# Decay arguments as one minimum, x times dt and the skip product on GpSimd, and an output product placed before the scores

## The chip, the cores and the metric

The kernel runs on one core of a Trainium2 chip, in one launch. The metric is the device time of one execution in microseconds; lower is better.

## The reference, cut to what matters

The program is a network of two layers over 1024 tokens of 512 values: attention, a linear layer, then a state space mixer (below), then an expert layer. The change is in the mixer and in the small tables that are made ahead of it. There are 128 heads of 64 values, in 8 groups, and the tokens are two sequences of 512.

```python
cum = jnp.cumsum(dA.reshape(b, nc, CS, H), axis=2)
Ldec = jnp.exp(cum[:, :, :, None, :] - cum[:, :, None, :, :])   # masked: j <= i
scores = jnp.einsum('bcihn,bcjhn->bcijh', Cc, Bc) * Ldec * dtc[:, :, None, :, :]
y_intra = jnp.einsum('bcijh,bcjhp->bcihp', scores, xc)
dlast = jnp.exp(cum[:, :, -1:, :] - cum)
states = jnp.einsum('bcjh,bcjhn,bcjhp->bchpn', dtc * dlast, Bc, xc)
y_inter = jnp.einsum('bcihn,bchpn->bcihp', Cc * jnp.exp(cum)[..., None], prev)
y = (y_intra + y_inter).reshape(b, l, H, P) + Dp[None, None, :, None] * x
...
g = y * jax.nn.silu(gate)
g = (gg * jax.lax.rsqrt(var + EPS)).reshape(b, l, INTER) * norm_w
return g @ out_w.T
```

## The kernel before, in words

The mixer works through 8 groups of heads, and each group through 16 steps. A step k takes 8 heads (half of a group) and one chunk of 128 tokens: half = k // 8 and c = k mod 8. Four chunks make a sequence. A step with c mod 4 not 0 carries a state in from the chunk before ("carrying"), one with c mod 4 not 3 feeds a state on. The steps of all groups are numbered through as s.

Each engine has a queue written out by hand, and semaphores order the queues against each other. In a step they do this:

- TensorE: the gate's product (into p_gate_intra), the product of the carried state (p_inter_state, L1668), the convolution's projection (p_mix) for the chunks that come later, the output product of the step before (p_out, 12 products of 128x512), the new state (L1682), the transposition of x (p_flip), the scores times x (L1693), and a product that sums the squares of the y of the step before (L1603, into the bank of p_inter_state). L102 is the line of a helper that issues all the large products.
- ScalarE: eight Exps of the decays (L1780), the high part of y (L1745), y's squares (L1751), the emptying of p_flip into x_tokens (L1738), the gate's and the convolution's activations and the convolution's first tap (L785).
- VectorE: `arguments(s + 1)` for the next step's decays (L1927), `skip_part` (L1973 and L1976), the state's decay and sum (L2036, L2075, L2077), the other three taps of the convolution (L807), `make_y` (y's sum L1984, times the gate L1989), the low part of y (L1937) and the reads of the sum of squares (L1944, L1946). In the first step of a half (c = 0) it also splits four pieces of the output weights (w_out, L1905).
- GpSimd: the decays times the scores of the chunk (`decayed`, L2156), x times the state's factors (`to_state`, L2147), the two sums of squares (L2131, L2133), the low parts of the gate's and the convolution's weights.

The matrix of a step and head holds exp(min(cum_i - cum_j, 0)) times dt_j. Before, VectorE formed the difference head by head, with one column of the table as minimum and subtrahend, and the logarithm of dt was the bias of the Exp. Ahead of the mixer, the tables of cum and of log dt are made and written; `end_logs` forms cum at the chunk's end minus cum plus log dt for the states, once a group.

In the last step of a half (c = 7) there is no new state and no transposition behind the convolution's products, and the output product of the step before stands behind the scores; in the other steps it stands ahead of the state.

## Time and profile before

| what | value |
|---|---|
| time, median of 3 runs | 2126.28 us (2123.61 to 2127.76) |
| time of the profiled execution | 2117.76 us |
| its span | 2115.8 us |
| granted TensorE clock, mean share | 0.982 |
| TensorE matmul busy | 1973.0 us (93%) |
| VectorE busy | 1797.9 us (85%) |
| ScalarE busy | 1447.2 us (68%) |
| GpSimd busy | 1054.1 us (50%) |

The span runs from the first to the last instruction in the trace, and the time is that of the whole execution. The mixer takes most of it, from about 402 to 2045 us of the span; a full group takes 205 us. Busy shares are means over the whole program, in which the stages ahead of the mixer and behind it have other limits. In rows of the trace, PE is TensorE, PEld its weight loads, DVE is VectorE, ACT is ScalarE and POOL is GpSimd; L and a number is the line of the kernel, and buffer numbers of tiles are left out, so that wq_t names the decays' buffer, p_gate_intra the bank of the gate's and of the scores' products, and p_inter_state that of the carried state, of the new state and of the sum of squares.

### The profile page before, as it was taken

Reading aid. Unit: us, or ns where it says so; the run is one execution under the profiler, and the core shown is the slowest. Engines: PE = TensorE matmul, PEld = TensorE weight load, DVE = VectorE, ACT = ScalarE, POOL = GpSimd, SP = SyncE. Lnnn points to the kernel's source line nnn. Section 1 sums busy time; section 2 is a strip of 40 time slices with the busy share of each in tenths; the row PEclk is TensorE's granted clock in tenths of the full one; section 3 lists DMA queues with packets and bytes.
Section 4 is the critical chain, followed back from the end, with each engine's and each line's share of the span. In section 5 each row is a group of like instructions: output and inputs, shape, how many; then the busy total and the mean of one; then the engine's idle time right before and its main releaser. Section 6 shows DMA issues by size and latency. Waiting matters only on the chain.

```text
span 2115.8 us, 34810 instructions
## 1 busy us (share of the span) xinstructions
PE 1973.0 (93%) x11288; PEld 1528.3 (72%) x11288; DVE 1797.9 (85%) x4144; ACT 1447.2 (68%) x2756; POOL 1054.1 (50%) x1033
## 2 busy tenths in 40 slices
PE   8899896799999999999999999999999999999878
PEld 4666575587777777777777777777777777777655
DVE  5777674589899989998998999989999998999976
ACT  1566624577778777777787777777877777877621
POOL 4555240245555555546554645465546555654541
PEclk9999997899999999999999999999999999999989
DMA  4000010233222313232323232223232322222201
GB/s 169 2 0 0 1 56 19 85 110 110 71 79 96 124 65 106 76 115 66 109 86 104 86 89 95 86 85 89 96 98 72 108 92 90 81 90 80 96 19 40
DMA packets 125713, 166.09 MB, mean 79 GB/s; under 512 B 37777, under 2 KB 88977, under 8 KB 121330
## 3 DMA queue, kind: packets, MB, share of 16 engines
q1 hardware_dynamic: 125554, 164.11, 24.2%
q8 instruction: 83, 1.36, 0.3%
q14 instruction: 76, 0.62, 0.1%
HBM read 159.88 MB, written 4.20 MB: 78 GB/s over the span
## 4 chain that ended last, share of the span: by engine, by line
DVE 30%; PE 27%; ACT 21%; issue 7%; POOL 2%; SPq 0%; DMA 0%; ACTq 0%; POOLq 0%; DVEq 0%
DVE conv L807 10%; PE p_mix L102 6%; PE p_out L102 6%; DVE wq_t L1927 6%; PE p_gate_intra L102 5%; ACT wq_t L1780 4%; ACT L1790 3%; ACT L1780 3%; DVE w_out L1905 2%; PE p_gate_intra L1693 2%; DVE x_skip L1976 2%; ACT conv L785 2%; POOL wq_t L2156 2%; ACT x_and_gate L1790 2%; DVE p_gate_intra L1984 2%
## 5 line engine op out<-in xcount | busy, mean ns | idle before, releaser
L2156 POOL TENSOR_TENSOR wq_t<-wq_t,cb 128x1024 f32<-128x1024 f32 x128 | 309.3, 2416 | 386.0 <-ACT wq_t L1780 374.8
L102 PE MATMUL p_out<-w_out,yT 128*128 128x512 f32 x1536 | 383.7, 400 | 11.2 <-DVE yT L1937 11.2
L1927 DVE TENSOR_SCALAR wq_t<-cum_all,tables_in 128x128 f32<-128x128 f32 x1024 | 359.2, 422 | 4.1 <-DMA cum_all<-cum_rows 4.1
L807 DVE SCALAR_TENSOR_TENSOR conv<-p_mix,unit_small,conv 128x511 f32<-128x511 f32 (+2 forms) x384 | 287.0, 748 | 83.9 <-ACT conv L785 72.8
L102 PE MATMUL p_gate_intra<-x_high,w_gate 128*128 128x512 f32 x1024 | 351.5, 404 | 6.1 <-ACT x_and_gate L1790 4.9
L102 PE MATMUL p_mix<-x_high,w_x 128*128 128x512 f32 x1024 | 351.6, 405 | 1.4 <-DVE x_low L1155 1.4
L102 PEld LDWEIGHTS p_out<-w_out,yT 128*128 128x128 f32 x1536 | 290.7, 191 | 82.6 <-DVE yT L1937 15.0
L1780 ACT ACTIVATE wq_t<-wq_t,tables_in 128x128 f32<-128x128 f32 x1024 | 326.1, 390 | 4.9 <-DVE wq_t L1927 3.4
L795 ACT ACTIVATE x_and_gate<-conv 128x512 f32<-128x512 f32 x128 | 80.9, 632 | 259.4 <-DVE conv L807 259.2
L102 PEld LDWEIGHTS p_gate_intra<-x_high,w_gate 128*128 128x128 f32 x1024 | 194.3, 190 | 45.6 <-issue 6.1
L102 PEld LDWEIGHTS p_mix<-x_high,w_x 128*128 128x128 f32 x1024 | 193.7, 189 | 39.9 <-DVE x_low L1155 1.8
L102 PE MATMUL p_gate_intra<-x_low,w_gate 128*128 128x512 f32 x512 | 201.8, 394 | 0.0
L102 PE MATMUL p_mix<-x_low,w_x 128*128 128x512 f32 x512 | 201.0, 393 | 0.0
L2147 POOL TENSOR_TENSOR x_to_state<-x_tokens,group_exps 128x512 f32<-128x512 f32 x96 | 101.2, 1054 | 171.1 <-ACT x_tokens L1738 171.1
L1693 PE MATMUL p_gate_intra<-wq_t,x_tokens 128*64 128x128 f32 x2048 | 140.9, 280 | 29.9 <-POOL wq_t L2156 29.9
L1780 ACT ACT_TABLE_LOAD x118 | 151.4, 1283 | 2.1
L1693 PEld LDWEIGHTS p_gate_intra<-wq_t,x_tokens 128*64 128x64 f32 x2048 | 109.9, 137 | 58.5 <-POOL wq_t L2156 36.6
L1790 ACT ACT_TABLE_LOAD x110 | 141.1, 1283 | 2.0
L826 POOL TENSOR_TENSOR w_x<-w_raw_tiles,w_x 128x512 fp32r<-128x512 f32 x64 | 83.0, 1297 | 112.9 <-DVE w_x L815 112.9
L476 DVE CUSTOM_DVE_ANT_0 pF<-pF,row_mask 128x128 f32<-128x128 f32 (+3 forms) x256 | 115.8, 530 | 18.5 <-PE pF L293 18.5
L1668 PEld LDWEIGHTS p_inter_state<-bc_channels,state 128*128 128x128 f32 x768 | 99.5, 194 | 43.6 <-issue 38.6
L1668 PE MATMUL p_inter_state<-bc_channels,state 128*128 128x128 f32 x768 | 105.3, 281 | 27.0 <-DVE mean_square L1946 17.5
(242 smaller groups left out, 4216.7 us busy)
## 6 DMA issues: line engine op xcount, KB each, us to landing
cum_all<-cum_rows SPq DMA_DIRECT2D x128, 512.0 KB, 3.8
exp_cum<-exp_rows SPq DMA_DIRECT2D x192, 128.0 KB, 3.4
w_staged<-in_w_gate SPq DMA_DIRECT2D x16, 1024.0 KB, 5.5
w_raw_tiles<-in_w_x SPq DMA_DIRECT2D x64, 256.0 KB, 3.0
w_staged<-in_w_out SPq DMA_DIRECT2D x16, 1024.0 KB, 4.9
w_raw_tiles<-in_w_bc SPq DMA_DIRECT2D x16, 256.0 KB, 5.3
x<-in_x SPq DMA_DIRECT2D x1, 2048.0 KB, 18.6
out<-x_and_gate SPq DMA_DIRECT2D x8, 256.0 KB, 2.0
```

The costliest lines, as they stand in the source:

```text
L102: last = pe.matmul(dst, left[a](k), right[b](k), start=k == 0 and n_ == 0, stop=stop and k == tiles - 1 and n_ == 2)
L476: m = dve.tensor_tensor_reduce(pF[:, b, n_ * wide:(n_ + 1) * wide], pF[:, b, n_ * wide:(n_ + 1) * wide], row_mask[:, CPS * P - wide:], 1.0 ...
L795: act.activation(dst, src, ACT.Silu).then_inc(self.conv_done, 1)
L807: m = dve.scalar_tensor_tensor(self.conv[:, par, back:], self.p_mix[:, bank, 0:SEQ - back], w[:, TAPS - 1 - back:TAPS - back], self.conv[: ...
L826: pool.tensor_tensor(self.wx[:, 1, j], self.raw[:, j % 2], self.wx[:, 0, j].bitcast(F32), ALU.subtract).then_inc(self.x_w_split, 1)
L1668: m = pe.matmul(p_inter[:, j * P:(j + 1) * P], state[:, 2 * j:2 * j + 2].rearrange("p h e -> p (h e)"), BC[:, 1, cols], start=True, stop=True)
L1693: m = pe.matmul(p_intra[a * HEAD_P:(a + 1) * HEAD_P, j * P:(j + 1) * P], xtok[:, k % 2, h], decay[:, k % 2, h], start=True, stop=True)
L1780: m = act.activation(decay[:, k % 2, h], decay[:, k % 2, h], ACT.Exp, bias=tab[:, s // STEPS % 2, 1, c, head:head + 1])
L1790: act.activation(tile_of(SG, phase, j), p_gate.rearrange("p (q t) -> p q t", t=P), ACT.Silu).then_inc(sg_done, 1)
L1927: m = dve.tensor_scalar(decay[:, k % 2, h], cumB[:, h], own, own, ALU.min, ALU.subtract)
L2147: pool.tensor_tensor(xs[:], xtok[:, k % 2], over(exps[:, 0, c, mine], HEAD_P), ALU.mult).then_inc(xs_done, 1)
L2156: pool.tensor_tensor(decay[:, k % 2], decay[:, k % 2], cb[:, c].unsqueeze(1).to_broadcast([P, UNIT_HEADS, P]), ALU.mult).then_inc(decay_do ...
```

## The change

- The argument of a step is one VectorE minimum of cum_i and cum_j over 128x1024 (8 heads); minus cum_j is the bias of the Exp. The table of log dt becomes one of dt, and the Ln that made it goes.
- dt is multiplied into x: GpSimd's `to_scores` forms x_dt from x_tokens in every step, and the scores' products take x_dt. The state's factors get dt from `dt_end`, once a group. x_tokens has one buffer in place of two.
- `end_logs` moves from VectorE to GpSimd, and also forms minus cum.
- GpSimd forms the skip product (x times D) in one operation, behind the decayed scores and ahead of the sums of squares. In carrying steps VectorE adds the carried part with one operation, `add_skip`, behind the taps (c below 7) or ahead of y's sum (c = 7). TensorE's carried product and sum of squares wait for that addition; before, they waited for `skip_part`.
- At c = 7 the output product of the step before stands ahead of the scores.

```diff
@@ layer 0's end: the tables @@
-                act.wait_ge(const2, 3)
-                act.wait_ge(stats_done, 4 * CHUNKS + 1)
-                act.activation(log_dt[:], dt[:], ACT.Ln, bias=head_small[:, 3:4]).then_inc(soft, 1)
...
@@ TensorE @@
-                                wait(pe, xskip_done, s)
+                                wait(pe, skip_sum, n_carries(g, k))
...
-                            if c < CHUNKS - 1:
-                                project_out(*before)
+                            project_out(*before)
...
-                        pe.wait_ge(flip_out, s + 1)
+                        pe.wait_ge(xdt_done, s + 1)
...
-                        if c == CHUNKS - 1:
-                            project_out(*before)
                         if before:
-                            wait(pe, xskip_done, s + 1)
+                            wait(pe, skip_sum, n_carries(g, k + 1))
                             square_sums(*before, p_inter)
@@ ScalarE @@
-                        m = act.activation(decay[:, k % 2, h], decay[:, k % 2, h], ACT.Exp, 
-                                           bias=tab[:, s // STEPS % 2, 1, c, head:head + 1])
+                        m = act.activation(decay[:, k % 2, h], decay[:, k % 2, h], ACT.Exp,
+                                           bias=neg[:, s // STEPS % 2, c, head:head + 1])
@@ VectorE @@
-                    for h in range(UNIT_HEADS):
-                        head = half * UNIT_HEADS + h
-                        own = tab[:, s // STEPS % 2, 0, c, head:head + 1]
-                        m = dve.tensor_scalar(decay[:, k % 2, h], cumB[:, h], own, own, ALU.min, ALU.subtract)
-                    m.then_inc(arg_done, 1)
-
-                end_logs(0)
+                    dve.tensor_tensor(decay[:, k % 2], cumB[:], over(tab[:, s // STEPS % 2, 0, c, mine], P),
+                                      ALU.min).then_inc(arg_done, 1)
...
-                            dve.wait_ge(carried_done, nc_ + 1)
-                            skip_part(g, k)
...
+                        def add_skip():
+                            if carries(c):
+                                dve.wait_ge(carried_done, n_carries(g, k) + 1)
+                                dve.wait_ge(xskip_done, s + 1)
+                                skipped = xskip[:].rearrange("p j t -> p (j t)")
+                                dve.tensor_tensor(skipped, p_inter[:], skipped, ALU.add).then_inc(skip_sum, 1)
...
                         if c == CHUNKS - 1:
+                            add_skip()
                             make_y(g, k)
                             taps_of(events)
...
+                        add_skip()
                         if feeds(c):
@@ GpSimd @@
+                def skip_part(g, k, first):
+
+                    half, c = divmod(k, CHUNKS)
+                    if c % CPS == 0:
+                        pool.wait_ge(conv_done, len(PLAN.first) if first and k == 0 else
+                                     PLAN.ready(g, k - 1, ("x", UT - 1, c // CPS)))
+                    wait(pool, y_sum, step(g, k))
+                    pool.tensor_tensor(xskip[:], chunk_of(X, c // CPS, c % CPS), over(skip[:, g % 2, half], P),
+                                       ALU.mult).then_inc(xskip_done, 1)
...
+                        def to_scores():
+                            wait(pool, intra_done, s)
+                            pool.tensor_tensor(xdt[:], xtok[:], over(tab[:, g % 2, 1, c, mine], HEAD_P),
+                                               ALU.mult).then_inc(xdt_done, 1)
+
+                        if k == 0:
+                            dt_end(g)
                         if c % CPS == 0:
-                            decayed()
+                            decayed(g, k)
+                        pool.wait_ge(flip_out, s + 1)
                         if feeds(c):
-                            pool.wait_ge(flip_out, s + 1)
                             to_state()
+                        to_scores()
+                        if not (first and k < 2) and older[1] >= CHUNKS:
+                            inverse_rms(*older)
                         if c % CPS:
-                            decayed()
+                            decayed(g, k)
+                        skip_part(g, k, first)
+                        if k == STEPS - 2 and not last:
+                            end_logs(g + 1)
                         if not (first and k == 0):
                             sum_squares(s - 1)
```

TensorE's queue at the last step of a half, from the last convolution product to the first gate product, before:

```order
L102 MATMUL p_mix<-x_low,w_x 128x512
L102 MATMUL p_mix<-x_high,w_x 128x512
L1693 MATMUL p_gate_intra<-wq_t,x_tokens 64x128 x8
L102 MATMUL p_out<-w_out,yT 128x512 x12
L1603 MATMUL p_inter_state<-one_column,y_squares 128x1
L102 MATMUL p_gate_intra<-x_high,w_gate 128x512
```

and after the change:

```order
L102 MATMUL p_mix<-x_low,w_x 128x512
L102 MATMUL p_mix<-x_high,w_x 128x512
L102 MATMUL p_out<-w_out,yT 128x512 x12
L1689 MATMUL p_gate_intra<-wq_t,x_dt 64x128 x8
L1600 MATMUL p_inter_state<-one_column,y_squares 128x1
L102 MATMUL p_gate_intra<-x_high,w_gate 128x512
```

The output product went from behind the scores to ahead of them; the scores' line is now L1689, and they take x_dt.

GpSimd's queue at the first step of the second half (k = 8), from the decays to the sums of squares of the step before, and on to the decays of k = 9, before:

```order
L2156 TENSOR_TENSOR wq_t<-wq_t,cb 128x1024
L2147 TENSOR_TENSOR x_to_state<-x_tokens,group_exps 128x512
L2131 TENSOR_TENSOR y_squares<-y_squares 128x256
L2133 TENSOR_TENSOR y_squares<-y_squares 128x128
L2147 TENSOR_TENSOR x_to_state<-x_tokens,group_exps 128x512
L2156 TENSOR_TENSOR wq_t<-wq_t,cb 128x1024
L2131 TENSOR_TENSOR y_squares<-y_squares 128x256
```

and after the change:

```order
L2110 TENSOR_TENSOR wq_t<-wq_t,cb 128x1024
L2151 TENSOR_TENSOR x_to_state<-x_tokens,group_dt_end 128x512
L2156 TENSOR_TENSOR x_dt<-x_tokens,tables_in 128x512
L2101 TENSOR_TENSOR x_skip<-x_and_gate,skip_in 128x512
L2137 TENSOR_TENSOR y_squares<-y_squares 128x256
L2139 TENSOR_TENSOR y_squares<-y_squares 128x128
L2151 TENSOR_TENSOR x_to_state<-x_tokens,group_dt_end 128x512
L2156 TENSOR_TENSOR x_dt<-x_tokens,tables_in 128x512
L2110 TENSOR_TENSOR wq_t<-wq_t,cb 128x1024
L2101 TENSOR_TENSOR x_skip<-x_and_gate,skip_in 128x512
```

x_dt (L2156 there, whose number before was that of the decays) and the skip product (L2101) came in ahead of the two sums of squares, which are L2137 and L2139 after.

VectorE's queue in step k = 9, a carrying one, from the arguments of the next step to y's sum, before:

```order
L1927 TENSOR_SCALAR wq_t<-cum_all,tables_in 128x128 x8
L1937 TENSOR_TENSOR yT<-p_gate_intra,yT 128x512
L2029 TENSOR_TENSOR p_inter_state<-p_inter_state,exp_cum 128x512
L1973 SCALAR_TENSOR_TENSOR x_skip<-x_and_gate,skip_in,p_inter_state 128x128 x4
L2036 TENSOR_TENSOR state<-state,group_exps 128x512
L819 CAST w_bc<-w_raw_tiles 128x512
L807 SCALAR_TENSOR_TENSOR conv<-p_mix,unit_small,conv 128x511
L807 SCALAR_TENSOR_TENSOR conv<-p_mix,unit_small,conv 128x510
L807 SCALAR_TENSOR_TENSOR conv<-p_mix,unit_small,conv 128x509
L2075 TENSOR_TENSOR state<-p_inter_state,state 128x512
L1984 TENSOR_TENSOR p_gate_intra<-p_gate_intra,x_skip 128x512
```

and after the change:

```order
L1910 TENSOR_TENSOR wq_t<-cum_all,tables_in 128x1024
L1919 TENSOR_TENSOR yT<-p_gate_intra,yT 128x512
L2001 TENSOR_TENSOR p_inter_state<-p_inter_state,exp_cum 128x512
L2006 TENSOR_TENSOR state<-state,group_exps 128x512
L819 CAST w_bc<-w_raw_tiles 128x512
L807 SCALAR_TENSOR_TENSOR conv<-p_mix,unit_small,conv 128x511
L807 SCALAR_TENSOR_TENSOR conv<-p_mix,unit_small,conv 128x510
L807 SCALAR_TENSOR_TENSOR conv<-p_mix,unit_small,conv 128x509
L2018 TENSOR_TENSOR x_skip<-p_inter_state,x_skip 128x512
L2048 TENSOR_TENSOR state<-p_inter_state,state 128x512
L1956 TENSOR_TENSOR p_gate_intra<-p_gate_intra,x_skip 128x512
```

The eight operations of the arguments became one (L1910), the four of the skip went from behind the carried product, and the addition L2018 stands behind the three taps, ahead of the state's sum (L2048) and y's sum (L1956).

## Rows read from the trace of the kernel before

**Rows 1.** Windows, two groups; columns as in the line on top.
```profile
core 0: us, PE busy (x) PEld busy (x) DVE busy (x) ACT busy (x) POOL busy (x), PEclk, DMA share, GB/s
980.03:1185.22 205.19, 198.50 (x1122) 157.70 (x1121) 187.79 (x401) 158.36 (x299) 113.69 (x95) 1.00 0.29 92
1390.38:1597.13 206.75, 199.96 (x1121) 158.82 (x1121) 187.88 (x401) 158.35 (x299) 113.73 (x95) 0.99 0.29 91
```

**Rows 2.** Timeline, TensorE, one group: start, us, engine, line, tiles, [idle before <-releaser].
```profile
1011.61 1.09 PE L1693 MATMUL p_gate_intra<-wq_t,x_tokens 128*64 128x128 f32 x16 [2.31 <-POOL wq_t L2156]
...
1034.16 1.13 PE L1668 MATMUL p_inter_state<-bc_channels,state 128*128 128x128 f32 x8 [0.71 <-DVE mean_square L1946]
...
1112.46 1.09 PE L1693 MATMUL p_gate_intra<-wq_t,x_tokens 128*64 128x128 f32 x16 [1.49 <-POOL wq_t L2156]
...
1132.13 1.13 PE L1668 MATMUL p_inter_state<-bc_channels,state 128*128 128x128 f32 x8 [1.17 <-DVE sum_squares L1944]
```

**Rows 3.** Costliest groups: busy us, mean ns of one | idle before.
```profile
L1927 DVE TENSOR_SCALAR wq_t<-cum_all,tables_in 128x128 f32<-128x128 f32 x1024 | 359.2, 422 | 4.1 <-DMA cum_all<-cum_rows 4.1
...
L2156 POOL TENSOR_TENSOR wq_t<-wq_t,cb 128x1024 f32<-128x1024 f32 x128 | 309.3, 2416 | 386.0 <-ACT wq_t L1780 374.8
...
L2147 POOL TENSOR_TENSOR x_to_state<-x_tokens,group_exps 128x512 f32<-128x512 f32 x96 | 101.2, 1054 | 171.1 <-ACT x_tokens L1738 171.1
...
L1973 DVE SCALAR_TENSOR_TENSOR x_skip<-x_and_gate,skip_in,p_inter_state 128x128 f32<-128x128 f32 x384 | 107.8, 343 | 3.4
```

**Rows 4.** Timeline, VectorE, ahead of the mixer and in a step.
```profile
356.34 1.23 DVE L1187 SCALAR_TENSOR_TENSOR dt<-dt,dt_abs 128x1024 f32<-128x1024 f32 x1 [8.48 <-ACT dt_abs L1102]
...
1035.11 2.14 DVE L1927 TENSOR_SCALAR wq_t<-cum_all,tables_in 128x128 f32<-128x128 f32 x8
```

**Rows 5.** Timeline, TensorE and VectorE, around the ends of two halves.
```profile
1018.78 2.92 PE L102 MATMUL p_out<-w_out,yT 128*128 128x512 f32 x12
...
1113.61 0.70 DVE L1984 TENSOR_TENSOR p_gate_intra<-p_gate_intra,x_skip 128x512 f32<-128x512 f32 x1 [2.32 <-PE p_gate_intra L1693]
...
1117.26 0.69 DVE L1937 TENSOR_TENSOR yT<-p_gate_intra,yT 128x512 fp32r<-128x512 f32 x1
...
1119.36 2.92 PE L102 MATMUL p_out<-w_out,yT 128*128 128x512 f32 x12
```

**Rows 6.** Timeline, VectorE, GpSimd and TensorE, first steps of two halves.
```profile
1024.71 2.73 DVE L1905 SCALAR_TENSOR_TENSOR w_out<-w_staged,unit_small,w_out 128x512 fp32r<-128x512 f32 x4
...
1024.78 2.97 POOL L2133 TENSOR_TENSOR y_squares<-y_squares 128x128 f32<-128x128 f32 x1
...
1123.99 3.70 DVE L1905 SCALAR_TENSOR_TENSOR w_out<-w_staged,unit_small,w_out 128x512 fp32r<-128x512 f32 x4 [0.95 <-ACT w_out L1729]
...
1124.43 1.18 POOL L2131 TENSOR_TENSOR y_squares<-y_squares 128x256 f32<-128x256 f32 x1
...
1126.71 1.09 PE L1693 MATMUL p_gate_intra<-wq_t,x_tokens 128*64 128x128 f32 x16
```

**Rows 7.** Timeline, ScalarE, VectorE and TensorE, step k = 9.
```profile
1138.15 0.77 ACT L785 ACTIVATE conv<-p_mix,unit_small 128x512 f32<-128x512 f32 x1
...
1139.69 2.30 DVE L807 SCALAR_TENSOR_TENSOR conv<-p_mix,unit_small,conv 128x511 f32<-128x511 f32 x3
...
1141.03 0.38 PE L1603 MATMUL p_inter_state<-one_column,y_squares 128*128 128x1 f32 x2
```

**Rows 8.** Timeline, ScalarE and TensorE, ahead of the mixer's first step.
```profile
358.45 1.15 ACT L1105 ACTIVATE dt<-dt,head_small 128x1024 f32<-128x1024 f32 x1 [2.14 <-DVE dt_abs L1189]
...
398.94 0.47 PE L102 MATMUL p_gate_intra<-x_high,w_gate 128*128 128x512 f32 x1 [2.50 <-ACT x_and_gate L1790]
```

**Rows 9.** Timeline, VectorE and TensorE, one of the last steps.
```profile
2002.48 4.51 DVE L1927 TENSOR_SCALAR wq_t<-cum_all,tables_in 128x128 f32<-128x128 f32 x8
...
2007.64 4.35 PE L102 MATMUL p_out<-w_out,yT 128*128 128x512 f32 x12 [3.67 <-DVE yT L1937]
```

**Rows 10.** Timeline, TensorE, an output product at a later half's end.
```profile
1422.99 4.62 PE L102 MATMUL p_out<-w_out,yT 128*128 128x512 f32 x12
```

More of the change, by code:

```diff
@@ L1964, in out_sum @@
                                              ALU.mult, ALU.add).then_inc(acc_done, 1)
-                def skip_part(g, k):
-                    half, c = divmod(k, CHUNKS)
-                    src = chunk_of(X, c // CPS, c % CPS)
-                    for j in range(UT):
-                        gain = skip[:, g % 2, half, j:j + 1]
-                        if carries(c):
-                            m = dve.scalar_tensor_tensor(xskip[:, j], src[:, j], gain, p_inter[:, j * P:(j + 1) * P],
-                                                         ALU.mult, ALU.add)
-                        else:
-                            m = dve.tensor_scalar(xskip[:, j], src[:, j], gain, None, ALU.mult)
-                    m.then_inc(xskip_done, 1)
                 def make_y(g, k):
```

80 lines of the change are left out of this document (39 added, 41 removed).

## The prediction

> **What bounds the kernel now.** I read the busy time by stage first, because the page's busy shares are means over stages with different limits. In one group of the mixer TensorE is busy 198.50 of 205.19 us [rows 1]; VectorE has 187.79, ScalarE 158.36 and GpSimd 113.69. TensorE is the bound, and a group can gain no more than 205.19 - 198.50 = 6.7 us. Then I read TensorE's own timeline through that group for its waits. Four of them carry most of the 6.7 [rows 2]: the scores wait for the decays on GpSimd at the two ends of a half (2.31 and 1.49), and the first carrying product of a half waits for VectorE's read of the mean square or the sum of squares (0.71 at k = 1, 1.17 at k = 9). Elsewhere in the group no wait of TensorE reaches 0.7. So time taken off VectorE is worth something only in so far as it reaches these four places, the start of the mixer, or its last steps.
>
> The profiled execution took 2117.76 us, with a span of 2115.8; the median of the runs shown is 2126.28, that is 8.5 more. The sum below is made against 2117.76 and then put on the median by adding its difference to 2126.28. About 0.2% (4 us) is what a measurement of this kernel can tell from no change.
>
> **The arguments.** Eight operations of 0.422 us become one minimum over 128x1024 [rows 3]. The nearest operation of that size with two SBUF inputs took 1.23 us; eight old ones undisturbed took 2.14 [rows 4]. Per step 359.2/128 = 2.81 becomes 1.23 to 1.6. In a steady group this is off the path: the Exps on ScalarE use arguments made a step earlier, and their number and form stay. Worth there: 0.
>
> **The skip term.** Four operations of 0.343 us [rows 3] leave VectorE in a carrying step, and one addition of 128x512 comes in (0.70 by the additions of that size [rows 5]). GpSimd gets one 128x512 product more for the skip, and another for x times dt. Priced by x_to_state, 1.054 us each [rows 3], this is 16 x 2.1 = 34 us in a group, on top of 113.7: 148 of 205, so GpSimd does not become the bound by its sum. The product with dt stands ahead of the decays in most steps, and the decays behind it wait 386.0/128 = 3.0 us a step for ScalarE anyway [rows 3], which covers its 1.05; ScalarE's copy into x_tokens, now one buffer, waits for the product of the step before, which is long past. Both at 0, unless that cover goes. The step without it is c = 0, where the decays stand first.
>
> **The half's end (c = 7).** Before, TensorE ends the convolution's products at 1112.46 - 1.49 = 1110.97 and begins the next step's output product at 1119.36: 8.4 us; at the group's end 1011.61 - 2.31 = 1009.30 to 1018.78: 9.5 [rows 2, 5]. After, the older output product (2.92) stands first and covers the wait for the decays; the scores follow (1.09); from their end at 1113.55 VectorE needs until 1117.26 + 0.69 = 1117.95, 4.4 us, to have y split [rows 5], with y's sum, gate, three taps and the split in a row. 2.92 + 1.09 + 4.4 = 8.4. The wait thus moves to the next output product, which no older product now covers. At k = 7 I get 0, at k = 15 a gain of 1.1: **-1.1 us a group**, bounds -3.8 (both waits gone) and 0.
>
> **The first step of a half (c = 0).** VectorE splits w_out in four operations while GpSimd works on the same step. At k = 8 the four took 3.70 us, with a sum of squares on GpSimd in between; at k = 0 they took 2.73 in one run, and a GpSimd operation of 128x128 beside them took 2.97 [rows 6]. So the two keep each other out, and at k = 8 VectorE lost 3.70 - 2.73 = 0.97 to it. After the change GpSimd has two operations of 1.05 more there, ahead of the two sums of squares. If they come in between the splits, the splits end up to 2.1 later. Behind the splits stand the taps, the state's copy, y and the read of the sum of squares, for which the carrying product of k = 9 waits already, so this delay lands on TensorE in full. One more GpSimd operation let in is +1.0, two are +2.1, none is 0. I take +1.0 at k = 8, because the two sums of squares then fall behind the splits. At k = 0 the splits go from 2.73 to 3.70 + 1.0 = 4.7, so 2.0 longer, but can begin 1.3 sooner (they start 5.93 after the output product there, 4.63 at k = 8 [rows 5, 6], as VectorE has less ahead of them): +0.7. Together **+1.7 us a group**, bounds -1.7 and +3.9.
>
> The Trainium skill ("SBUF — State Buffer", section "SBUF: two separate sides") says that a VectorE operation with two SBUF inputs and a GpSimd operation take a shared pair of ports in turn as an exclusive lock, each for its whole instruction. By that rule all of GpSimd's new operations would alternate with the splits, and the +1.7 would be +3.9. The trace agrees at k = 8 and not at k = 0, where VectorE went through four operations in a row.
>
> **The sums of squares.** The product that sums y's squares writes into the bank that the skip term is added from, so it waits for the new addition, which stands behind the step's taps; before, it waited for the skip operations ahead of the taps. At k = 9 it ran at 1141.03 while the taps ended at 1139.69 + 2.30 = 1141.99 [rows 7]. After the change VectorE reaches the taps sooner, but ScalarE's first tap ends only at 1138.15 + 0.77 = 1138.92: taps to 1141.2, addition to 1141.9, so TensorE waits 0.9. What is queued behind on TensorE is the gate's product, and behind that everything. In the other steps TensorE is later against the taps; I put them at 0.3 together, from 0 to 2. **+1.2 us a group**.
>
> **Sum in the groups.** -1.1 + 1.7 + 1.2 = +1.8. The first and last of eight groups have only part of this: 7.5 x 1.8 = +13.5.
>
> **Ahead of the mixer.** The Ln of dt goes (1.15, with ScalarE on the path [rows 8]): -1. The first gate product after the convolution's waits 2.50 for ScalarE [rows 8], which waited for the first arguments; one operation in place of eight, and the end logs on another engine, take up to 2.5 off, but the end logs now stand on GpSimd ahead of the gate weights: -2. **-3**, bounds 0 and -5.
>
> **The last steps.** With no further group to prepare, TensorE is not full. The output product waits 3.67 us for y's split, which stands behind arguments that took 4.51 [rows 9]; the same pair comes once more some 17 us later. The arguments become 1.23 alone, or 3.4 if GpSimd's two new operations keep them out: -1.1 to -3.3, I take -2.3 twice, and -1.4 for the output product ahead of the last scores, near the 1.49 of the half's end [rows 2]. **-6**, bounds -2 and -10.
>
> **In all** 13.5 - 3 - 6 = +4.5 us: 2122 in an execution like the profiled one, and on the median **2131**.
>
> **The rivals.**
> *A, the sum above*: 45%. Its own range is 2121 to 2141.
> *B, VectorE keeps the upper hand at c = 0*: the splits run as at k = 0 (2.73, GpSimd kept out, [rows 6]). Then k = 0 loses its wait of 0.71. At k = 8 x times dt comes only after 1123.99 + 2.73 + 1.05 = 1127.8, where the scores ran at 1126.71 [rows 6], so the scores lose 1.1 and this eats the 1.17 gained at k = 9. The taps are 1.0 sooner, and the 0.9 at the sum of squares goes. A group is -1.1 - 0.7 - 0.1 + 0.2 = -1.7, times 7.5 is -13, with -9 outside -22: 2104. For it: the row of 2.97; against it: the 3.70 at k = 8, where GpSimd came in. It decides at one GpSimd operation fewer between the splits. 30%.
> *C, all four waits go*: 7.5 x 6.7 = 50, and 9 outside: 2067. Against it: y's chain of 4.4 has nothing taken out. 5%.
> *D, the new waits lower TensorE's clock*: after the 2.31 wait at the end of one half the output product ran 4.62 instead of 2.92 [rows 10], and that group took 206.75 instead of 205.19 [rows 1]. With 1.6 more at both halves of a group, 15 times, 24 comes on top of A: 2155. Against it: the other waits of this length left the clock alone. 10%.
> *E, nothing of it is seen*: gains at start and end are as large as the losses, 7.5 x 1.2 = 9 against 9, or hidden: 2126. 10%.
>
> **The numbers.** B, C and the lower end of A (0.06) are faster: 0.41. E and the middle of A (0.15) are the same: 0.25. D and the upper part of A (0.24) are slower: 0.34. The range reaches to B and into D, 2100 to 2150, and leaves out C, most of D and a little of B.
>
> **What would show it.** In the profile after: the minimum at 1.2 to 1.6 us; no wait of the scores for the decays at c = 7, but one of the output product for y's split in the next step; the four w_out splits at 4 to 5 us in both halves; the sum of squares waiting about 0.9 for the new addition at k = 9; group times of 206 to 208 us. Splits of 2.7 us and groups near 203.5 would show B. What would make it wrong most easily is the placing of GpSimd's two new operations against VectorE's, at c = 0 and in the steps where I put their effect at nothing.

## The result and the profile after

The changed kernel took 2147.55 us (median of 4, 2144.84 to 2151.23) against 2127.02 us of the kernel before (median of 4): a ratio of 1.0102 (95% interval 1.0090 to 1.0114), 20.5 us slower. The prediction was 2131, +4.5, with a range of 2100 to 2150. The side and the range were right; the size was a quarter of what was measured, and 2147.55 lies outside the 2121 to 2141 that the prediction gave to its own sum. The side was in part luck: by the prediction's own chances "faster" (0.41) stood ahead of "slower" (0.34).

The page's busy line after the change, as a whole:

```profile
span 2146.7 us, 33910 instructions
PE 1986.8 (93%) x11288; PEld 1542.5 (72%) x11288; DVE 1601.3 (75%) x2815; ACT 1445.1 (67%) x2755; POOL 1391.0 (65%) x1313
```

VectorE lost 197 us of work and GpSimd took on 337. The kernel is nevertheless slower, because TensorE is the bound and it waits longer.

The spans of the two profiled executions differ by 30.9 us, ten more than the medians. Part of that lies ahead of everything that was changed. The timeline of TensorE shows one product of the linear layer that precedes the mixer's tables, and then the mixer's first scores, before:

```profile
305.59 0.39 PE L102 MATMUL pM<-w_lin_low,srcT 128*128 128x512 f32 x1
...
416.32 1.09 PE L1693 MATMUL p_gate_intra<-wq_t,x_tokens 128*64 128x128 f32 x16
```

and after:

```profile
315.61 0.39 PE L102 MATMUL pM<-w_lin_low,srcT 128*128 128x512 f32 x1
...
423.78 1.09 PE L1689 MATMUL p_gate_intra<-wq_t,x_dt 128*64 128x128 f32 x16
```

Ten us are lost ahead of that product, where the code is the same; the shown execution of before was a quick one there, and it also lies 8.5 under the median of before. What the change did is the other 20.9, and that is the difference of the medians.

A group of the mixer (windows; busy us and instructions of each engine, granted clock, DMA share, GB/s):

```profile
1672.33:1880.69 208.36, 199.43 (x1121) 159.18 (x1120) 163.49 (x235) 158.23 (x298) 155.85 (x130) 0.99 0.29 90
```

A group went from 205.19 [rows 1] to 208.36 us, +3.2, and eight of them make 25. TensorE was idle 6.7 us in it before and is idle 8.9 now; the other 0.9 is that its products take 199.4 in place of 198.5, in this group at a lower clock for a part of it (below). These are its waits in that group, from its timeline:

```profile
1678.18 1.13 PE L1665 MATMUL p_inter_state<-bc_channels,state 128*128 128x128 f32 x8 [1.12 <-DVE mean_square L1928]
...
1712.14 0.38 PE L1600 MATMUL p_inter_state<-one_column,y_squares 128*128 128x1 f32 x2 [1.62 <-DVE x_skip L2018]
...
1763.66 3.04 PE L102 MATMUL p_out<-w_out,yT 128*128 128x512 f32 x12 [1.26 <-DVE yT L1919]
...
1773.87 0.35 PE L1600 MATMUL p_inter_state<-one_column,y_squares 128*128 128x1 f32 x2 [1.65 <-issue]
...
1787.83 0.38 PE L1600 MATMUL p_inter_state<-one_column,y_squares 128*128 128x1 f32 x2 [0.45 <-DVE x_skip L2018]
...
1813.78 0.38 PE L1600 MATMUL p_inter_state<-one_column,y_squares 128*128 128x1 f32 x2 [0.62 <-DVE x_skip L2018]
...
1870.54 2.99 PE L102 MATMUL p_out<-w_out,yT 128*128 128x512 f32 x12 [1.99 <-DVE attn L1937]
```

Against [rows 2]: the scores' waits for the decays (2.31 and 1.49) are gone, and the output products of the next step wait in their place (1.26 for y's split at k = 8, 1.99 at the next group's k = 0, there for VectorE's read of the output product before). The sum of squares, which waited for nobody, waits at k = 3, 8, 9 and 11.

Behind the wait of 1.65 the granted clock was at its lower level (1.2 GHz) for a part of the gate's products. In an earlier group the same wait (1.66) left the clock at 2.4 GHz. The same products there and here (windows, columns as above):

```profile
730.71:734.52 3.81, 2.99 (x14) 2.18 (x14) 3.63 (x8) 2.10 (x4) 0.44 (x1) 1.00 0.00 0
1774.09:1778.51 4.42, 4.42 (x15) 3.47 (x15) 4.24 (x8) 2.71 (x4) 1.05 (x2) 0.61 0.00 0
```

At the upper level the products are done sooner, and the carried product of k = 9 then waits 3.81 - 2.99 = 0.82 for VectorE; after it the sum of squares waits 0.95 instead of 0.45:

```profile
744.44 0.38 PE L1600 MATMUL p_inter_state<-one_column,y_squares 128*128 128x1 f32 x2 [0.95 <-DVE x_skip L2018]
```

So a group at the upper level throughout has 10.3 us of waits and one like the group shown has 8.9 and slower products, and both take 208.4.

The new operations, from the costliest groups (busy us, mean ns | idle before):

```profile
L1910 DVE TENSOR_TENSOR wq_t<-cum_all,tables_in 128x1024 f32<-128x1024 f32 x128 | 211.7, 1654 | 4.1 <-DMA cum_all<-cum_rows 3.1
L2156 POOL TENSOR_TENSOR x_dt<-x_tokens,tables_in 128x512 f32<-128x512 f32 x128 | 179.7, 1404 | 27.0 <-ACT x_tokens L1731 23.9
L2101 POOL TENSOR_TENSOR x_skip<-x_and_gate,skip_in 128x512 f32<-128x512 f32 x128 | 155.0, 1211 | 0.0
```

All three are longer than the rows of before let expect (1.23, 1.05, 1.05), because VectorE and GpSimd keep each other out. The first step of the second half shows it (timeline of VectorE and GpSimd):

```profile
1762.66 2.39 POOL L2110 TENSOR_TENSOR wq_t<-wq_t,cb 128x1024 f32<-128x1024 f32 x1 [5.01 <-ACT wq_t L1774]
...
1763.59 2.55 DVE L1910 TENSOR_TENSOR wq_t<-cum_all,tables_in 128x1024 f32<-128x1024 f32 x1
...
1768.41 5.05 DVE L1899 SCALAR_TENSOR_TENSOR w_out<-w_staged,unit_small,w_out 128x512 fp32r<-128x512 f32 x4 [2.28 <-ACT w_out L1723]
...
1768.85 1.49 POOL L2156 TENSOR_TENSOR x_dt<-x_tokens,tables_in 128x512 f32<-128x512 f32 x1
...
1770.30 1.48 POOL L2101 TENSOR_TENSOR x_skip<-x_and_gate,skip_in 128x512 f32<-128x512 f32 x1
1771.75 1.16 POOL L2137 TENSOR_TENSOR y_squares<-y_squares 128x256 f32<-128x256 f32 x1
```

The minimum starts during the decays and ends 1.09 us after they end at 1765.05. The four splits of w_out take 5.05 (3.70 before, [rows 6]), and GpSimd's three operations take 1.2 to 1.5 each beside them: they take turns. The sums of squares come behind both, which is TensorE's wait of 1.65 at 1773.87.

The Trainium skill ("SBUF — State Buffer", section "SBUF: two separate sides") has a VectorE operation with two SBUF inputs and a GpSimd operation that reads SBUF shut each other out for a whole instruction, whichever starts first. These rows agree with that. The four splits at k = 0, which took 2.73 in every group of the kernel before, take 4.6 here in every group but the first.

### The profile page after: what moved, and what is told of

Read it like the earlier page. It is cut to its first block, busy times and chain, and to the rows that moved or that the text cites. A ratio compares the mean times of both kernels' runs of the same rounds, so it can differ in the third digit from the quotient of the medians.

```text
span 2146.7 us, 33910 instructions
## 1 busy us (share of the span) xinstructions
PE 1986.8 (93%) x11288; PEld 1542.5 (72%) x11288; DVE 1601.3 (75%) x2815; ACT 1445.1 (67%) x2755; POOL 1391.0 (65%) x1313
## 3 DMA queue, kind: packets, MB, share of 16 engines
q1 hardware_dynamic: 125554, 164.11, 23.9%
## 4 chain that ended last, share of the span: by engine, by line
PE 53%; DVE 17%; ACT 12%; issue 4%; POOL 1%; SPq 0%; DMA 0%; ACTq 0%; POOLq 0%; DVEq 0%
PE p_mix L102 13%; PE p_out L102 12%; PE p_gate_intra L102 12%; DVE conv L807 8%; PE p_gate_intra L1689 4%; DVE w_out L1899 3%; PE p_inter_state L1665 3%; ACT wq_t L1774 2%; PE p_inter_state L1678 2%; PE pM L102 2%; PE p_flip L1583 2%; ACT L1774 2%; ACT L1784 1%; PE p_inter_state L1600 1%; ACT conv L785 1%
## 5 line engine op out<-in xcount | busy, mean ns | idle before, releaser
L2110 POOL TENSOR_TENSOR wq_t<-wq_t,cb 128x1024 f32<-128x1024 f32 x128 | 331.2, 2587 | 235.0 <-ACT wq_t L1774 203.2
L102 PEld LDWEIGHTS p_out<-w_out,yT 128*128 128x128 f32 x1536 | 292.6, 192 | 96.6 <-issue 16.6
L102 PE MATMUL p_gate_intra<-x_high,w_gate 128*128 128x512 f32 x1024 | 355.8, 409 | 5.8 <-POOL w_gate L2083 3.4
L1774 ACT ACTIVATE wq_t<-wq_t,minus_cum 128x128 f32<-128x128 f32 x1024 | 326.0, 390 | 1.4
L1910 DVE TENSOR_TENSOR wq_t<-cum_all,tables_in 128x1024 f32<-128x1024 f32 x128 | 211.7, 1654 | 4.1 <-DMA cum_all<-cum_rows 3.1
L2156 POOL TENSOR_TENSOR x_dt<-x_tokens,tables_in 128x512 f32<-128x512 f32 x128 | 179.7, 1404 | 27.0 <-ACT x_tokens L1731 23.9
L2151 POOL TENSOR_TENSOR x_to_state<-x_tokens,group_dt_end 128x512 f32<-128x512 f32 x96 | 107.3, 1117 | 118.4 <-ACT x_tokens L1731 118.4
L2101 POOL TENSOR_TENSOR x_skip<-x_and_gate,skip_in 128x512 f32<-128x512 f32 x128 | 155.0, 1211 | 0.0
L1689 PE MATMUL p_gate_intra<-wq_t,x_dt 128*64 128x128 f32 x2048 | 140.1, 279 | 0.0
L1689 PEld LDWEIGHTS p_gate_intra<-wq_t,x_dt 128*64 128x64 f32 x2048 | 109.2, 136 | 27.7 <-issue 27.7
```

The source lines that it names most:

```text
L102: last = pe.matmul(dst, left[a](k), right[b](k), start=k == 0 and n_ == 0, stop=stop and k == tiles - 1 and n_ == 2)
L1689: m = pe.matmul(p_intra[a * HEAD_P:(a + 1) * HEAD_P, j * P:(j + 1) * P], xdt[:, h], decay[:, k % 2, h], start=True, stop=True)
L1774: m = act.activation(decay[:, k % 2, h], decay[:, k % 2, h], ACT.Exp, bias=neg[:, s // STEPS % 2, c, head:head + 1])
L1910: dve.tensor_tensor(decay[:, k % 2], cumB[:], over(tab[:, s // STEPS % 2, 0, c, mine], P), ALU.min).then_inc(arg_done, 1)
L2101: pool.tensor_tensor(xskip[:], chunk_of(X, c // CPS, c % CPS), over(skip[:, g % 2, half], P), ALU.mult).then_inc(xskip_done, 1)
L2110: pool.tensor_tensor(decay[:, k % 2], decay[:, k % 2], cb[:, c].unsqueeze(1).to_broadcast([P, UNIT_HEADS, P]), ALU.mult).then_inc(decay_do ...
```

## The experiments

Each was timed in turn with the kernel before, in five rounds; the ratios are to that. "The changed kernel" is the one above.

**Output product behind the scores again**

```diff
-                            project_out(*before)
+                            if c < CHUNKS - 1:
+                                project_out(*before)
...
                         m.then_inc(intra_done, 1)
+                        if c == CHUNKS - 1:
+                            project_out(*before)
```

> The changed kernel (2147.6 us) with only the output product put back behind the scores at c = 7. Theory: the reorder is about neutral, since it trades the scores' waits for the decays (3.8 us a group before) for waits of the next output product (1.26 and 1.99 us a group in the changed kernel); so 2144 to 2154 us, and the waits for the decays are back in the trace. Rival: the reorder itself costs, because the product now waits behind VectorE's read of the one before; then 2132 to 2140 us.

Measured: 2132.88 us, ratio 1.0028 (1.0017 to 1.0039), 14.7 us below the changed kernel. The rival's range was right; the theory was right only in that waits for the decays come back, and they are fewer than it had them. The view of waits (engine, tile and line waited for: us in all, times, longest) has for TensorE in the changed kernel

```profile
PE p_inter_state L1600 <- DVE x_skip L2018: 23.9, 32, 1.6
...
PE p_out L102 <- DVE attn L1937: 13.9, 7, 2.0
PE p_out L102 <- DVE yT L1919: 12.3, 11, 1.3
```

and without the reorder

```profile
PE p_inter_state L1600 <- DVE x_skip L2021: 24.1, 32, 1.7
...
PE p_gate_intra L1690 <- POOL wq_t L2113: 11.3, 9, 2.2
...
PE p_out L102 <- DVE yT L1922: 2.2, 3, 0.8
```

The output products lose 24 of 26 us of waiting, and the scores wait 11.3 us for the decays, not the 29.9 that they waited before the change: at k = 7 not at all, at k = 15 for 1.28. The other parts of the change had already brought the decays forward, so the reorder had little left to cover: per group it puts 1.26 + 1.99 of waits in the place of 1.28.

**Skip term on VectorE again, reorder kept**

```diff
-                                wait(pe, skip_sum, n_carries(g, k))
+                                wait(pe, xskip_done, s)
...
+                            dve.wait_ge(carried_done, nc_ + 1)
+                            skip_part(g, k)
...
-                        add_skip()
...
-                        skip_part(g, k, first)
```

> The changed kernel with the skip term back on VectorE in its four operations ahead of the taps, TensorE waiting for those as before; the minimum, x times dt on GpSimd and the reorder stay. Theory: the skip's move is the larger part of the loss, through the sum of squares that waits for the addition behind the taps (about 1.7 us a group) and through one GpSimd operation fewer beside the w_out splits (about 1 us a group): 2122 to 2132 us. Rival: x times dt on GpSimd is what costs, by keeping VectorE out of its port: 2140 us or more.

Measured: 2130.94 us, ratio 1.0018 (1.0008 to 1.0028), 16.6 us below the changed kernel. The theory holds for the skip's move as a whole.

**The minimum alone, on the kernel before**

```diff
+                    dve.tensor_tensor(neg[:, g % 2], tab[:, g % 2, 1], tab[:, g % 2, 0], ALU.subtract).then_inc(logs_done, 1)
...
+                    dve.tensor_tensor(decay[:, k % 2], cumB[:], over(tab[:, s // STEPS % 2, 0, c, mine], P),
+                                      ALU.min).then_inc(arg_done, 1)
```

> The kernel before (2127 us) with the one minimum alone: dt stays in the exponent, the bias of the Exp is log dt minus cum from one more 128x128 subtraction a group; no x times dt, no move of the skip term or of the output product. Theory: TensorE is the bound, so the minimum gives only what it takes off the start, the last steps and the first step of a half: 2112 to 2122 us. Rival: the arguments on VectorE are hidden everywhere: 2124 to 2130 us.

Here log dt is added to minus cum in single precision, where a large cum rounds it off, so this kernel computes with a changed dt; its time is that of the same operations. Measured: 2115.37 us, ratio 0.9944 (0.9930 to 0.9958), as the theory had it. By the traces the last group gives 6.8 us of it (188.3 to 181.5) and the six full groups 4.3 together.

**Sums of squares ahead of the skip product at c = 0**

```diff
-                        skip_part(g, k, first)
+                        if c:
+                            skip_part(g, k, first)
...
                             sum_squares(s - 1)
+                        if not c:
+                            skip_part(g, k, first)
```

> The changed kernel with GpSimd's skip product behind the sums of squares in the first step of a half only. Theory: the order of GpSimd's operations beside the w_out splits sets the wait at k = 8 (1.65 us at the sum of squares in the changed kernel); the splits end about 0.7 us sooner there: 2138 to 2144 us. Rival: the splits are kept out for as long by whatever GpSimd does next: within 3 us of 2147.6.

Measured: 2143.58 us, ratio 1.0078 (1.0064 to 1.0092), 4 us below the changed kernel. The waits of 1.65 at the sum of squares go, and 1.7 come back at the next carried product, which waits for VectorE behind the splits.

**The same without the reorder** (this edit and the first together)

> The changed kernel without the reorder (2132.9 us), with the skip product behind the sums of squares in the first step of a half; the addition stays behind the taps. Theory: the skip's move costs in two places, beside the w_out splits (some 4 us in all, as in the kernel with the reorder, 2147.6 to 2143.6) and through the sum of squares that waits for the addition (the rest): 2127 to 2131 us, which leaves some 13 us of the 18 to 2115 for the addition's place. Rival: the first step of a half is the larger part: 2115 to 2122 us.

Measured: 2123.57 us, ratio 0.9988 (0.9979 to 0.9997), 9.3 us below the kernel without the reorder alone. It lies between the two expectations: the first step of a half is worth about as much as the place of the addition.

**Minimum, x times dt and end logs alone** (the edits of the first two experiments together)

> The changed kernel without the reorder at c = 7 and with the skip term on VectorE as before: what stays of the change is the minimum, x times dt and the end logs on GpSimd. Theory: the two losses lie in different places (the output product's waits at c = 7; the sum of squares and the w_out splits elsewhere), so they add: 2147.6 - 14.7 - 16.6 = 2116, from 2112 to 2121 us, near the minimum alone (2115.4). Rival: both take from the same slack, or x times dt costs on its own: 2124 us or more.

Measured: 2115.00 us, ratio 0.9948 (0.9935 to 0.9961). The two losses add up (2147.6 - 14.7 - 16.6 = 2116), so the reorder and the skip term's move are what makes the changed kernel slower, and x times dt on GpSimd costs nothing that can be seen beside the 2115.4 of the minimum alone. What is left of the waits for the decays in a group (timeline):

```profile
1735.19 1.09 PE L1690 MATMUL p_gate_intra<-wq_t,x_dt 128*64 128x128 f32 x16 [0.90 <-POOL wq_t L2110]
...
1840.16 1.09 PE L1690 MATMUL p_gate_intra<-wq_t,x_dt 128*64 128x128 f32 x16 [1.72 <-POOL wq_t L2110]
```

**Addition of the skip term ahead of the taps, no reorder**

```diff
+                        add_skip()
                         if c == 0 and not (first and k == 0):
                             out_low_part(g * 2 + half, half)
                         taps_of(events)
...
-                        add_skip()
```

> The changed kernel without the reorder (2132.9 us), with the addition of the skip term ahead of the taps instead of behind them; GpSimd's order is untouched. Theory: the place of the addition makes the sum of squares wait (24 us in all in that kernel), so 2117 to 2125 us. Rival: the addition now waits for GpSimd's skip product, which stands behind the decays, and holds the taps back: 2130 us or more.

Measured: 2246.47 us, ratio 1.0561 (1.0546 to 1.0576). The rival, and by far more than it said: VectorE's waits have

```profile
DVE x_skip L2021 <- POOL x_skip L2104: 258.4, 96, 3.4
```

that is 2.7 us in each of the 96 carrying steps, with the taps and all of the next step's x behind it. The place behind the taps is the dear one for TensorE and the safe one for VectorE.

**And GpSimd's skip product ahead of the decays**

```diff
                         if c % CPS:
+                            skip_part(g, k, first)
                             decayed(g, k)
-                        skip_part(g, k, first)
+                        elif c:
+                            skip_part(g, k, first)
...
+                        if not c:
+                            skip_part(g, k, first)
```

> As the kernel with the addition ahead of the taps, and GpSimd's skip product ahead of the decays where these wait for ScalarE anyway, and behind the sums of squares in the first step of a half. Theory: with the skip product ready early nothing waits for it, and VectorE keeps the time it was spared: 2108 to 2118 us. Rival: the decays come 1.05 us later and the scores wait for them at c = 7: 2120 to 2132 us.

Measured: 2134.94 us, ratio 1.0038 (1.0024 to 1.0051): the waits of the sum of squares for the addition are gone, and the decays are late instead, as the rival said; the time is 3 us above the rival's range.

**The same, but behind the decays at c = 7**

```diff
-                        if c % CPS:
+                        if c % CPS and c < CHUNKS - 1:
                             skip_part(g, k, first)
                             decayed(g, k)
                         elif c:
+                            if c % CPS:
+                                decayed(g, k)
                             skip_part(g, k, first)
```

> The kernel with the skip product ahead of the decays (2134.9 us), but at c = 7 behind them. Theory: its wait of the scores for the decays at the group's end (2.66 us, and the output product at the lower clock behind it) comes from the skip product ahead of the decays at that step, and goes: 2110 to 2122 us. Rival: the decays are late there because ScalarE is, whatever stands ahead of them on GpSimd: 2130 us or more.

Measured: 2120.79 us, ratio 0.9973 (0.9961 to 0.9985). The scores at the group's end, in the kernel with the skip product ahead of the decays everywhere:

```profile
1854.38 1.36 PE L1690 MATMUL p_gate_intra<-wq_t,x_dt 128*64 128x128 f32 x16 [2.66 <-POOL wq_t L2113]
```

and in this one:

```profile
1838.63 1.09 PE L1690 MATMUL p_gate_intra<-wq_t,x_dt 128*64 128x128 f32 x16 [1.66 <-POOL wq_t L2113]
```

The output product behind these scores takes 4.31 us there and 3.03 here; its clock is shown in the last section. One GpSimd operation ahead of the decays costs 1.0 of waiting and then 1.3 at the lower clock. The theory holds. Even so, it is 6 us more than with the skip term on VectorE (2115.0).

**The reorder alone, on the kernel before**

```diff
-                            if c < CHUNKS - 1:
-                                project_out(*before)
+                            project_out(*before)
...
-                        if c == CHUNKS - 1:
-                            project_out(*before)
```

> The kernel before (2127 us) with the reorder at c = 7 alone. Theory: there the decays are late by 1.5 to 2.3 us at that place, so the reorder covers a wait that exists and gives it back as waits of the next output product: neutral, 2121 to 2130 us. Rival: it costs as in the changed kernel, where it was worth 14.7 us: 2136 to 2144 us.

Measured: 2131.3 us, ratio 1.0025 (1.0014 to 1.0035): a loss of about 5 us, just outside the theory's range and well short of the rival's. The windows of the six full groups and of the last one, before (first two lines) and with the reorder:

```profile
618.54:1851.11 1232.57, 1192.18 (x6721) 947.30 (x6720) 1126.44 (x2400) 950.17 (x1788) 682.37 (x564) 1.00 0.29 92
1851.11:2039.38 188.27, 160.71 (x911) 126.56 (x910) 168.64 (x363) 126.91 (x248) 89.55 (x78) 0.93 0.24 80
625.81:1861.04 1235.23, 1196.11 (x6721) 947.63 (x6720) 1121.27 (x2401) 949.03 (x1788) 669.70 (x564) 1.00 0.29 91
1861.04:2053.29 192.25, 166.07 (x922) 130.35 (x922) 169.47 (x364) 127.08 (x248) 91.96 (x80) 0.93 0.24 78
```

A full group goes from 205.4 to 205.9 on the mean, so there the theory nearly held. The last group loses 4.0, with one output product more in it than before; 1.1 of that comes back behind its last scores (75.3 us to the end, from 76.4).

**x times dt on VectorE, from the bank** (on the kernel with minimum and x times dt)

```diff
-                    act.activation(xtok[:].rearrange("p h e -> p (h e)"), p_flip[:], ACT.Copy).then_inc(flip_out, 1)
...
+                    dve.tensor_tensor(xdt[:], p_flip[:].rearrange("p (h e) -> p h e", e=HEAD_P),
+                                      over(tab[:, g % 2, 1, c, mine], HEAD_P), ALU.mult).then_inc(xdt_done, 1)
...
-                            pool.tensor_tensor(xs[:], xtok[:], over(dtend[:, c, mine], HEAD_P),
+                            pool.tensor_tensor(xs[:], xdt[:], over(exps[:, 0, c, mine], HEAD_P),
```

> The kernel with the minimum and x times dt alone (2115.0 us), with x times dt formed by VectorE straight from the transposed x in its bank, so that ScalarE's copy and one GpSimd operation a step go, and the state's factor is multiplied into that. Theory: ScalarE and GpSimd, which make the decays late at c = 7, lose 0.6 and 1.05 us a step, and VectorE gains 0.7: 2104 to 2114 us. Rival: VectorE's product stands behind y's gate and is waited for by TensorE or GpSimd: 2118 us or more.

Measured: 2080.41 us, ratio 0.9781 (0.9767 to 0.9794). This is 46 us below the kernel before, the best of all, and some 24 us below the theory's range, so the theory's prices do not explain it. A group of this kernel (windows, columns as above):

```profile
1621.86:1822.02 200.16, 197.13 (x1122) 158.07 (x1121) 172.60 (x303) 151.68 (x282) 122.22 (x96) 1.00 0.30 94
```

TensorE's idle time in a group is 3.0 us, from 6.7 in the kernel before.

**The same with ScalarE's copy back**

```diff
+                    act.activation(xtok[:].rearrange("p h e -> p (h e)"), p_flip[:], ACT.Copy).then_inc(flip_out, 1)
...
-                    dve.wait_ge(flip_done, step(g, k) + 1)
+                    dve.wait_ge(flip_out, step(g, k) + 1)
...
-                    dve.tensor_tensor(xdt[:], p_flip[:].rearrange("p (h e) -> p h e", e=HEAD_P),
+                    dve.tensor_tensor(xdt[:], xtok[:],
```

> The fastest kernel so far (2080.4 us), but with ScalarE's copy of the transposed x back, and VectorE's product with dt reading that copy instead of the bank. Theory: ScalarE, which is on the way to the decays, is what the copy's removal relieved, and most of the 35 us between 2115.0 and 2080.4 goes again: 2100 to 2118 us. Rival: taking the product off GpSimd was worth it, and ScalarE's copy is hidden: 2080 to 2092 us.

Measured: 2114.91 us, ratio 0.9958 (0.9945 to 0.9972). The theory's range is right: without the copy's removal, taking the product off GpSimd is worth nothing. Its reason, ScalarE on the way to the decays, is not what the traces show. TensorE's waits with the copy back:

```profile
PE p_inter_state L1664 <- DVE mean_square L1930: 29.6, 24, 5.0
...
PE p_inter_state L1678 <- POOL x_to_state L2160: 12.1, 17, 1.7
...
PE p_gate_intra L1689 <- POOL wq_t L2125: 7.3, 16, 1.5
```

and without it:

```profile
PE p_inter_state L1663 <- DVE mean_square L1918: 19.9, 10, 5.0
...
PE p_gate_intra L1688 <- POOL wq_t L2113: 5.2, 8, 1.8
...
PE p_inter_state L1677 <- POOL x_to_state L2148: 1.0, 1, 1.0
```

The waits for the state's x (11.1) and for VectorE's mean square (9.7) go with the copy, and those for the decays by only 2.1. The two kernels also differ in VectorE's product itself, which reads the bank or x_tokens (costliest groups, without the copy and with it):

```profile
L1960 DVE TENSOR_TENSOR x_dt<-p_flip,tables_in 128x512 f32<-128x512 f32 x128 | 87.3, 682 | 9.5 <-PE p_flip L1581 9.5
L1972 DVE TENSOR_TENSOR x_dt<-x_tokens,tables_in 128x512 f32<-128x512 f32 x128 | 129.6, 1013 | 21.1 <-ACT x_tokens L1733 20.9
```

Whether it is ScalarE's 0.6 us a step, the shorter way from the transposed x to the scores and the state, or the 0.33 that VectorE's product is shorter from the bank is not told apart; all three go with the copy.

## Why the prediction was right and wrong, point by point

**The bound and the form of the sum** were right: TensorE bounds the groups, VectorE's spared 197 us are worth nothing by themselves, and the time is made at a handful of waits.

**The arguments** came out at 1.65 on the mean, just above the 1.6 given, and GpSimd in a group at 155.9 instead of 148, both for taking turns. The minimum alone gains 11.7 us (2127 to 2115.4), of which 0.7 on the mean in a full group, where 0 was forecast. Nothing else of the change helps on balance.

**The half's end** was mis-sized, by half a microsecond a group. The term was -1.1 a group; the waits there went from 2.31 + 1.49 to 1.26 + 1.99, which is -0.55. The wait moved to the next output product as forecast. But at k = 15 I let that product wait for y's split alone. It also waits for VectorE to read the one before (the wait of 1.99), which stands behind y's split in VectorE's queue. And the question of what the half's end would be without the reorder was not asked. The wait to be covered was taken from the trace of before, but the decays were to come earlier by the change's other parts: without the reorder they are late by 0 and 1.28, not 1.49 and 2.31. So the reorder by itself cost 14.7 us in the changed kernel, and about 5 in the kernel before, where half of it lies in the last group.

**The first step of a half** was predicted at +1.7 a group, with splits of 4.7. The splits take 5.05 at k = 8, and 4.58 at k = 0 (3.70 and 2.73 before). The waits of a full group at the upper clock give +1.7 as well: 1.66 at k = 8 and 0.82 at k = 9 where 1.17 was, and 1.16 at k = 1 where 0.77 was. GpSimd's new operations did come in between the splits in both halves, which the prediction priced at up to +3.9; the splits grew by 1.35 and 1.86. That this agrees so closely is luck: the second half has 1.3 of it and the first 0.4, for 1.0 and 0.7, and the mechanism was in part another. At k = 8 the sum of squares waits (1.65) for GpSimd's sums, which stand behind the new products, and the carried product of k = 9 then waits less or not at all. The wait that I named comes back (1.7) when the sums are put first; without the reorder that order is worth 9.3 us, 1.2 a group.

**The sums of squares** are the step that failed in the groups: 1.2 was predicted, with 0.9 at k = 9 and 0.3 in all other steps together (from 0 to 2), for which no rows were read. At k = 9 the wait is 0.95 at the upper clock, as predicted. But it is 0.22 at k = 1, 1.61 at k = 3 and 0.60 at k = 11, that is 2.4 for the 0.3; over the program the waits on the addition are 23.9 us. About 1.0 of this takes the place of old waits at k = 4 and 13, so the term is +2.4 a group instead of +1.2. Against the skip term on VectorE the net loss is less: the kernel with the sums first and no reorder takes 2123.6 and the one with the skip term on VectorE 2115.0, which is 8.6 or 1.1 a group. In their traces the waits on the addition, less those that they replace, are 2.3 a group, and the waits for the decays at the half's ends are 1.3 shorter (1.3 against 0.9 + 1.7). What VectorE was spared did bring the decays forward, and the place of the addition cost more.

**Ahead of the mixer**: -3 was predicted. From the product in the linear layer to the first scores it is now 423.78 - 315.61 = 108.2 us; before it was 416.32 - 305.59 = 110.7. That is -2.5.

**The last steps** are the other step that failed: -6 was predicted, with -2.3 twice and -1.4 for the output product ahead of the last scores. The pair came out. From the scores at 1996.54 to those at 2031.91 it was 35.4 us, and it is now 30.2 (2029.96 to 2060.13), which is -5.2; its output products wait 0.83 instead of 3.67 [rows 9]:

```profile
2039.09 5.32 PE L102 MATMUL p_out<-w_out,yT 128*128 128x512 f32 x12 [0.83 <-DVE yT L1919]
```

The last half's end did not. Before:

```profile
2039.38 1.97 PE L1693 MATMUL p_gate_intra<-wq_t,x_tokens 128*64 128x128 f32 x16 [1.97 <-POOL wq_t L2156]
```

and after:

```profile
2066.17 3.83 PE L102 MATMUL p_out<-w_out,yT 128*128 128x512 f32 x12
2069.94 1.09 PE L1689 MATMUL p_gate_intra<-wq_t,x_dt 128*64 128x128 f32 x16
```

The wait of 1.97 is gone, but the output product that stands in its place runs 3.83 us, partly at the lower clock. From the scores before these to the last scores it is 9.8 us (2060.13 to 2069.94), from 7.5; and what stands behind the last scores is no shorter for it (76.8 us, from 76.4). That is +2.7 for the -1.4, and in all -2.5 for -6.

**In all**, the mixer takes 1646.2 us from its first to its last scores, from 1623.1. Its six full groups and its last one after the change (windows; those of before stand with the reorder alone):

```profile
628.94:1880.69 1251.75, 1194.21 (x6721) 952.83 (x6720) 979.72 (x1405) 949.28 (x1788) 935.09 (x775) 0.99 0.28 90
1880.69:2069.94 189.25, 166.29 (x923) 131.32 (x922) 149.78 (x216) 127.01 (x248) 129.51 (x109) 0.94 0.25 79
```

The six full groups give +19.2, the first +2.9 and the last +1.0. With -2.5 ahead of the mixer and +0.4 behind it that is 21.0, against the 20.9. Without the last steps the groups make 26, for the 13.5 predicted. Of the rivals, B did not happen (splits of 5.05), and C neither. D's lower clock did come: ahead of the last group it was there four times in the execution shown, once before. But only one group became longer by it, by 1.6 us, as one did before; in the other three the slower products took the place of waits.

## What to carry to other kernels

Cost a reorder that covers a wait against the wait as the rest of the change will leave it, not as the old trace shows it, and follow what the moved operation waits for in its new place: here the decays were hardly late any more, and the reorder cost 15 us. Work moved to an engine with spare time still has a place in that engine's queue; the skip product was late behind the decays and made the decays late ahead of them, and both were dearer than four operations on the busier engine. The largest gain came from one pass less over the same data: x times dt formed straight from the bank by VectorE, with ScalarE's copy gone, gained three times what the minimum did. What ended by it were mainly TensorE's waits for the state's x and for VectorE's mean square; which part of the edit ended them was not told apart.

## What the runs showed of the hardware

VectorE and GpSimd took turns whole instructions long, even for a plain cast (timeline of the changed kernel, k = 9):

```profile
1781.71 2.95 POOL L2110 TENSOR_TENSOR wq_t<-wq_t,cb 128x1024 f32<-128x1024 f32 x1 [1.22 <-ACT wq_t L1774]
1782.30 2.65 DVE L819 CAST w_bc<-w_raw_tiles 128x512 fp32r<-128x512 f32 x1
```

The cast has one SBUF input, and took 2.65 us, until 0.3 after the decays' end. And TensorE's granted clock fell after a single wait, though not each time. In the kernel with the skip product ahead of the decays everywhere, the window of the output product that follows the wait of 2.66 us (columns as above; the granted clock is third from the end)

```profile
1855.68:1860.00 4.32, 4.32 (x17) 3.51 (x16) 3.54 (x5) 1.06 (x4) 1.52 (x2) 0.68 0.00 0
```

and the same product after the wait of 1.66, in the kernel with it behind them at c = 7:

```profile
1839.65:1842.70 3.05, 3.05 (x17) 2.54 (x16) 2.78 (x5) 2.32 (x7) 2.76 (x4) 1.00 0.01 4
```

The first ran partly at 1.2 GHz, the second at 2.4 throughout. In the first kernel this came in six of the seven groups ahead of the last, in the second in none. In the changed kernel the wait of 1.65 at k = 8 was followed by the lower clock in three of seven groups. Before, a wait of 2.31 in the same place left the clock alone in one group [rows 2] and was followed by a slow product in another [rows 10].
